# Local attention in the stream: two-bank reads, one exponent a tile, group products ahead of the scores

## What is computed

```python
x = x + attn_a(layernorm(x));  x = x + ffn(layernorm(x))
x = x + attn_b(layernorm(x));  x = x + ffn(layernorm(x))

def layer(x, wqkv, qs, ksc, wo, lg, lb, w1, b1, w2, b2):   # 8 heads of 64, window 64
    q, k, v = heads(shift_token(x) @ wqkv)
    q, k = rotary_xpos(l2norm(q) * qs, l2norm(k) * ksc)
    # each window of 64 queries sees its own 64 keys and the 64 before, masked
    attn = softmax(where(mask, -big, (8 * q) @ k.T))
    x = x + (attn @ v) @ wo
    h = layernorm(shift_token(x)) * lg + lb
    a, g = split(h @ w1 + b1)                               # 341 columns each
    return x + (a * gelu(g)) @ w2 + b2
```

## Time and profile before

| | |
|---|---|
| median of three runs | 1033.52 us |
| lowest and highest | 1033.38 and 1034.92 us |
| profiled execution, its own time | 1037.81 us |
| span of its trace | 1036.0 us |
| mean granted TensorE clock (share of full) | 0.979 |
| TensorE busy | 958.6 us (93%) |
| TensorE weight loads busy | 585.5 us (57%) |
| VectorE busy | 735.3 us (71%) |
| ScalarE busy | 736.7 us (71%) |
| GpSimd busy | 387.5 us (37%) |

### The profile page before, as it was taken

How to read it: one execution, slowest core, us unless ns; L and a number is a source line. 1 busy time by engine, 2 the same in 40 slices (tenths; PEclk the granted TensorE clock), 3 DMA queues, 4 the chain that set the end, 5 groups by cost and what they waited for, 6 DMA issues and landing times.

```text
span 1036.0 us, 22905 instructions
## 1 busy us (share of the span) xinstructions
PE 958.6 (93%) x8720; PEld 585.5 (57%) x8720; DVE 735.3 (71%) x1218; ACT 736.7 (71%) x1568; POOL 387.5 (37%) x270
## 2 busy tenths in 40 slices
PE   5999999998789999999998998989899999999985
PEld 2333333333576667666665566656666676666752
DVE  3787887884687877777776667757677777776741
ACT  3477777777587787877866675767668778787762
POOL 3010113000656545455443433424263553634410
PEclk9999999999899999999999998999999999999998
DMA  2200000000411101011010000000010100111100
GB/s 69 66 15 1 2 2 2 2 2 2 119 26 23 27 17 32 18 27 22 18 29 9 22 17 14 21 15 22 7 32 17 28 22 17 32 28 26 33 22 11
DMA packets 23303, 23.72 MB, mean 23 GB/s; under 512 B 8626, under 2 KB 15068, under 8 KB 23196
## 3 DMA queue, kind: packets, MB, share of 16 engines
q1 hardware_dynamic: 23196, 22.27, 9.1%
HBM read 6.16 MB, written 1.05 MB: 7 GB/s over the span
## 4 chain that ended last, share of the span: by engine, by line
PE 62%; DVE 7%; ACT 2%; issue 2%; POOL 2%; DVEq 0%; POOLq 0%
PE psum L1267 8%; PE psum L1236 5%; PE psum L1176 5%; PE psum L1197 5%; PE psum L1148 5%; PE psum L1138 5%; PE psum L1186 4%; PE psum L1275 4%; PE psum L1140 4%; PE psum L1139 4%; PE psum L1260 3%; PE psum L1209 2%; PE psum L1254 2%; PE psum L1161 2%; DVE f_PT L1530 2%
## 5 line engine op out<-in xcount | busy, mean ns | idle before, releaser
L1067 POOL TENSOR_TENSOR f_A<-f_A,f_BS 128x1024 f32<-128x1024 f32 x64 | 151.0, 2360 | 222.6 <-DVE f_BS L1506 222.4
L743 DVE TENSOR_REDUCE a_M<-psum 128x2 f32<-128x1024 f32 x128 | 155.6, 1222 | 41.0 <-PE psum L547 40.3
L1072 POOL TENSOR_TENSOR f_A<-f_A,f_RN 128x1024 f32<-128x1024 f32 x64 | 121.8, 1903 | 91.1 <-ACT f_RN L1398 87.4
L675 ACT ACTIVATE a_PT<-psum 128x1024 f32<-128x1024 f32 x128 | 128.7, 1023 | 24.9 <-PE psum L557 24.4
L1383 ACT ACTIVATE f_PW<-psum,f_NM 128x128 f32<-128x128 f32 x512 | 138.4, 380 | 4.2 <-DVE f_NM L1538 4.2
L1538 DVE TENSOR_REDUCE f_NM<-psum 128x4 f32<-128x512 f32 x128 | 82.3, 685 | 68.0 <-PE psum L1176 66.8
L1349 ACT ACTIVATE f_SQ<-psum 128x512 f32<-128x512 f32 x128 | 75.3, 608 | 71.5 <-PE psum L1140 67.0
L1502 DVE TENSOR_TENSOR f_A<-psum,cos 128x512 f32<-128x512 f32 x128 | 87.8, 686 | 45.2 <-ACT f_SQ L1349 45.1
L1197 PE MATMUL psum<-f_VS,f_PT 128*64 128x65 f32 x1024 | 81.2, 228 | 32.5 <-DVE f_hidden L1585 13.8
L1197 PEld LDWEIGHTS psum<-f_VS,f_PT 128*64 128x64 f32 x1024 | 67.8, 139 | 65.5 <-issue 48.4
L1267 PE MATMUL psum<-f_mid,f_w 128*128 128x512 f32 (+1 forms) x192 | 86.5, 601 | 2.7 <-DVE f_mid L1568 2.7
(11 more groups left out here) (191 smaller groups left out, 1948.7 us busy)
## 6 DMA issues: line engine op xcount, KB each, us to landing
f_VS<-f_V SPq DMA_DIRECT2D x112, 130.0 KB, 2.3
raw<-L_ffn_wqkv_dram SPq DMA_DIRECT2D x2, 768.0 KB, 5.4
a_XT<-L_attn_a_x_dram SPq DMA_DIRECT2D x4, 256.0 KB, 2.9
out_dram<-f_OUT SPq DMA_DIRECT2D x4, 256.0 KB, 2.3
f_w<-L_ffn_w_dram SPq DMA_DIRECT2D x2, 341.0 KB
tables<-const_dram SPq DMA_DIRECT2D x1, 512.0 KB, 3.8
f_wo<-L_ffn_wo_dram SPq DMA_DIRECT2D x8, 64.0 KB
const<-const_dram SPq DMA_DIRECT2D x1, 264.0 KB, 3.0
```

What stands on the lines that cost most here:

```text
L675: nc.scalar.activation(PT[:, i % 4, :, :], psum[:, pair("by_key", i), :], ACT.Exp, scale=float(DA) ** -0.5).then_inc(s("exped"), 1)
L743: nc.vector.tensor_reduce(M[:, quads % 2, t, 2 * j:2 * j + 2], psum[:, pair("scores", i), :], AX_X, ALU.max).then_inc(s("maxed"), 1)
L1067: nc.gpsimd.tensor_tensor(A[:, k % 2, :, :], A[:, k % 2, :, :], BS[:, k % 2, :, :], ALU.add)\
L1072: nc.gpsimd.tensor_tensor(x, x, RN[:, k % 2, :, None].to_broadcast([P, 2 * HW, DW]), ALU.mult)\
```

## The change

Four things are changed in the stream.

- Softmax: VectorE takes the maxima of both score banks in one instruction and then adds the negated maxima to the scores of both banks, into SBUF (f_PW). ScalarE computes the exponent of the whole tile in place, in one instruction of 1024 columns without a bias. The score banks come free when VectorE's addition is done.
- Copies: q and k transposed, and the two transposed banks of exponents, are each copied by one ScalarE instruction over two neighbouring banks. VectorE's copy (1530) is gone, and turn_p_2 with it. For this the bank list skips bank 7 where a pair would straddle the end (28 skips). q is kept in the same tile as k.
- Division: one reciprocal and one multiplication for both banks of sums, and one semaphore increment for a tile's sums.
- Order: w1, w2 and wo come before the scores on TensorE, turn_p before turn_o on TensorE and ScalarE, norm before w1 on ScalarE, and w1, wo and w2 before soften on VectorE. All three blocks of w1 are one stage again on VectorE.

```diff
-           ("turn_o", 3, of_tile), ("w1", 5, of_group), ("turn_p", 2, of_tile),
+           ("turn_p", 2, of_tile), ("turn_o", 3, of_tile),
...
+           ("w1", 5, of_group), ("w2", 6, of_group), ("wo", 3, of_group), ("scores", 1, of_tile),
...
+    def together(first, second):
+
+        if len(order) % BANKS == BANKS - 1:
+            order.append(None)
+        order.extend((first, second))
+
...
-            order += [("turned_q", i), ("turned_k", i)]
-        elif stage in ("scores", "sums", "keys_b", "tokens_b"):
-            order += [(stage, 2 * i), (stage, 2 * i + 1)]
-        elif stage in ("turn_p", "turn_p_2"):
-            order += [("turn_p", 2 * i + (stage == "turn_p_2"))]
+            together(("turned_q", i), ("turned_k", i))
+        elif stage in ("scores", "sums", "keys_b", "tokens_b", "turn_p"):
...
+    def two_banks(first, second):
+
+        x, y = bank(*first), bank(*second)
+        assert y == x + 1
+        return psum[:, x:y + 1, :]
...
-             "turned_q": ("qk_copied", lambda i: 2 * i + 1), "turned_k": ("qk_copied", lambda i: 2 * i + 2),
-             "scores": ("exped", lambda i: i + 1), "turn_p": (("p_copied", "p_copied_2"), lambda i: i // 2 + 1),
-             "sums": ("divided", lambda i: i + 1), "turn_o": ("o_copied", lambda i: i + 1),
+             "turned_q": ("qk_copied", lambda i: i + 1), "turned_k": ("qk_copied", lambda i: i + 1),
+             "scores": ("lowered", lambda i: i // 2 + 1), "turn_p": ("p_copied", lambda i: i // 2 + 1),
+             "sums": ("divided", lambda i: i // 2 + 1), "turn_o": ("o_copied", lambda i: i + 1),
...
-                def turn_p(u):
-                    pe.wait_ge(s("exped"), u + 1)
-                    dst = take("turn_p", u)
-                    for c in range(PAIRS):
-                        last = nc.tensor.transpose(dst[:, P * c:P * c + P], PW[:, u % 4, c, :], g.ident)
-                    last.then_inc(s("turned_p"), 1)
+                def turn_p(k):
+                    pe.wait_ge(s("exped"), k + 1)
+                    for u in (2 * k, 2 * k + 1):
+                        dst = take("turn_p", u)
+                        for c in range(PAIRS):
+                            last = nc.tensor.transpose(dst[:, P * c:P * c + P], PW[:, u % 4, c, :], g.ident)
+                        last.then_inc(s("turned_p"), 1)
...
-                        nc.scalar.activation(QT[:, k % 2, :, :],
-                                             psum[:, bank("turned_q", k), :].rearrange("p (c x) -> p c x", c=PAIRS),
-                                             ACT.Copy).then_inc(s("qk_copied"), 1)
-                        act.wait_ge(s("turned"), 2 * k + 2)
-                        nc.scalar.activation(KT[:, :, 2 * t:2 * t + 2, :],
-                                             psum[:, bank("turned_k", k), :].rearrange("p (c s x) -> p c s x",
-                                                                                       c=PAIRS, s=2),
+                        of_q = TILES + k % 2
+                        both = KT[:, :, :, :].rearrange("p c (u s) x -> p u c (s x)", s=2)
+                        both = both[:, of_q:t - 1:t - of_q, :, :] if t else both[:, of_q::-of_q, :, :]
+                        nc.scalar.activation(both,
+                                             two_banks(("turned_q", k), ("turned_k", k))
+                                             .rearrange("p w (c x) -> p w c x", c=PAIRS),
                                              ACT.Copy).then_inc(s("qk_copied"), 1)
...
-                        for u in (2 * i, 2 * i + 1):
-                            act.wait_ge(s("maxed"), u + 1)
-                            if u >= 4:
-                                act.wait_ge(s("turned_p"), u - 3)
-                            for c in range(PAIRS):
-                                last = nc.scalar.activation(PW[:, u % 4, c, :],
-                                                            psum[:, bank("scores", u), P * c:P * c + P], ACT.Exp,
-                                                            bias=NM[:, u % 4, c:c + 1])
-                            last.then_inc(s("exped"), 1)
+                        k = i
+                        act.wait_ge(s("lowered"), k + 1)
+                        of = slice(2 * (k % 2), 2 * (k % 2) + 2)
+                        nc.scalar.activation(PW[:, of, :, :], PW[:, of, :, :], ACT.Exp).then_inc(s("exped"), 1)
...
-                        u = 2 * i
-                        act.wait_ge(s("turned_p"), u + 1)
-                        if u >= 4:
-                            act.wait_ge(s("sums"), u - 3)
-                        nc.scalar.activation(PT[:, u % 4, :, :],
-                                             psum[:, bank("turn_p", u), :].rearrange("p (c x) -> p c x", c=PAIRS),
+                        k = i
+                        act.wait_ge(s("turned_p"), 2 * k + 2)
+                        if k >= 2:
+                            act.wait_ge(s("sums"), k - 1)
+                        nc.scalar.activation(PT[:, 2 * (k % 2):2 * (k % 2) + 2, :, :],
+                                             two_banks(("turn_p", 2 * k), ("turn_p", 2 * k + 1))
+                                             .rearrange("p j (c x) -> p j c x", c=PAIRS),
                                              ACT.Copy).then_inc(s("p_copied"), 1)
...
-                    elif stage == "turn_p_2":
-                        u = 2 * i + 1
-                        dve.wait_ge(s("turned_p"), u + 1)
-                        if u >= 4:
-                            dve.wait_ge(s("sums"), u - 3)
-                        nc.vector.tensor_copy(PT[:, u % 4, :, :],
-                                              psum[:, bank("turn_p", u), :].rearrange("p (c x) -> p c x", c=PAIRS))\
-                          .then_inc(s("p_copied_2"), 1)
                     elif stage == "soften":
-                        dve.wait_ge(s("scores"), i + 1)
-                        for u in (2 * i, 2 * i + 1):
-                            if u >= 4:
-                                dve.wait_ge(s("exped"), u - 3)
-                            nc.vector.tensor_reduce(
-                                NM[:, u % 4, :], psum[:, bank("scores", u), :].rearrange("p (c x) -> p c x", c=PAIRS),
-                                AX_X, ALU.max, negate=True).then_inc(s("maxed"), 1)
+                        k = i
+                        dve.wait_ge(s("scores"), k + 1)
+                        if k >= 2:
+                            dve.wait_ge(s("lowered"), k - 1)
+                        of = slice(2 * (k % 2), 2 * (k % 2) + 2)
+                        x = two_banks(("scores", 2 * k), ("scores", 2 * k + 1)).rearrange("p j (c x) -> p j c x", c=PAIRS)
+                        nc.vector.tensor_reduce(NM[:, of, :], x, AX_X, ALU.max, negate=True).then_inc(s("maxed"), 1)
+                        dve.wait_ge(s("maxed"), k + 1)
+                        if k >= 2:
+                            dve.wait_ge(s("turned_p"), 2 * k - 2)
+                        nc.vector.tensor_tensor(PW[:, of, :, :], x, NM[:, of, :, None].to_broadcast([P, 2, PAIRS, P]),
+                                                ALU.add).then_inc(s("lowered"), 1)
                     elif stage == "sums":
-                        for u in (2 * i, 2 * i + 1):
-                            x = psum[:, bank("sums", u), 0:PAIRS * (DW + 1)].rearrange("p (c x) -> p c x", c=PAIRS)
-                            dve.wait_ge(s("sums"), u + 1)
-                            nc.vector.reciprocal(RD[:, u % 4, :], x[:, :, DW]).then_inc(s("den_recip"), 1)
-                            dve.wait_ge(s("den_recip"), u + 1)
-                            if u >= 4:
-                                dve.wait_ge(s("turned_o"), u // 2 - 1)
-                            nc.vector.tensor_tensor(ON[:, u % 4, :, :], x[:, :, 0:DW],
-                                                    RD[:, u % 4, :, None].to_broadcast([P, PAIRS, DW]), ALU.mult)\
-                              .then_inc(s("divided"), 1)
+                        k = i
+                        of = slice(2 * (k % 2), 2 * (k % 2) + 2)
+                        x = two_banks(("sums", 2 * k), ("sums", 2 * k + 1))[:, :, 0:PAIRS * (DW + 1)]
+                        x = x.rearrange("p j (c x) -> p j c x", c=PAIRS)
+                        dve.wait_ge(s("sums"), k + 1)
+                        nc.vector.reciprocal(RD[:, of, :], x[:, :, :, DW]).then_inc(s("den_recip"), 1)
+                        dve.wait_ge(s("den_recip"), k + 1)
+                        if k >= 2:
+                            dve.wait_ge(s("turned_o"), k - 1)
+                        nc.vector.tensor_tensor(ON[:, of, :, :], x[:, :, :, 0:DW],
+                                                RD[:, of, :, None].to_broadcast([P, 2, PAIRS, DW]), ALU.mult)\
+                          .then_inc(s("divided"), 1)
```

66 lines of the change are left out of this document (33 added, 33 removed).

## The result

The changed kernel takes **1083.0 us** (median of 4 runs, 1082.66 to 1083.87) against 1033.5: ratio **1.0454**, 95% interval 1.0425 to 1.0483, slower. The forecast was 1063 us in a range of 1038 to 1085.

What follows compares the result with a forecast made beforehand. TensorE's list order was taken as the bound. Output steps +30.4, norm +6.5, up -9.7, linear-attention groups +2, fill and end +1 gave +30 us: 1068 profiled, 1063 as median; own range 1048 to 1076, whole range 1038 to 1085.

Steps and rivals of the forecast that it cites:

- the clock falls: Rival: most of the 8 long output-step stalls are each followed by a half-clock stretch, +14, 1077 us; chance 0.17.
- the linear groups get worse: Rival: each linear-attention group is +5 us through bank waits that chain, 1081 us; chance 0.08.
- What bounds it: TensorE's list order sets a plain group's time; work off ScalarE or VectorE is worth only what TensorE waits for it.
- Loop and output step: Scores to squares, then turn_o's copy: output product stalls 2.15 us, 3.2 behind a first layer's down step; +30.4 us in all.
- 1.2 us or less: Sign of being wrong: an output product that waits no longer than this for turn_o's copy.
- Norm and up steps: Plain groups: norm steps slower by 1.0 (5) or 0.25 (6), +6.5 us; up steps -0.5 (4) or -1.1 (7), -9.7 us.
- the down step: Down step of plain groups: no change, 0, as f_hidden is ready and the exponents end before turn_p's place.
- The end with its last plain group: End of the stream: the forecast gave the fill and the end together about +1 us.
- The linear-attention groups: Four groups: old waits and half clock go, new waits of 8 us against 7.5 before; +0.5 each, +2 us.
- The faster one: Rival: waits go, nothing replaces them, output product waits only 1.2 us, linear groups -6.4 each; -32, 1002 us; chance 0.13.

Runs made afterwards that it cites:

- experiment 1: All new operations, with the engine lists in the order of the kernel before and turn_p whole in front of the scores: 1039.25 us, 1.0032 to before.
- 2: Kernel before with its old operations, in the new order of the changed kernel: 1041.56 us, ratio 1.0050 to before.
- 7: New operations in the old order, with ScalarE's squares ahead of the exponents: 1031.42 us, ratio 0.9964 to the kernel before.
- 9: Kernel before with its own operations; on VectorE alone the tokens' division and all of w1 moved ahead of the maxima: 1023.25 us, ratio 0.9857.
- 8: New operations in the old order, squares ahead of the exponents, and VectorE's division of the tokens ahead of the maxima: 1020.08 us, 0.9848 to the kernel before.

## Why the prediction was right, and where its size was off

- **Direction and mechanism right, size too small.** +29.5 us were forecast and +49.5 measured. The time lies 2 us inside the upper bound of the range (1085) and outside the forecast's own, 1048 to 1076. By the time alone the rivals "the clock falls" (1077) and "the linear groups get worse" (1081) fit better; the lengths of the steps and the list of waits are what speaks for the forecast.
- **What bounds it.** Right. TensorE's list order set the time; 56 us taken off ScalarE bought nothing, and the 47 us of experiment 1, in the old order, bought nothing either. The prediction had allowed this up to 45 us of gain, at 0.02. (ScalarE's work fell by 0.88 us a tile where 0.7 was said, VectorE's rose by 0.26 where 0.2 was said.)
- **Loop and output step.** Right in mechanism and size. The exponents were to be ready at 3.6 us behind a first layer's down step, and were at 3.62; turn_o's copy at 7.65, and ended at 7.40; 3.05 and 2.0 us more a step were said, 3.0 and 2.1 measured. The loss isn't one wait of 3.2 us at the product, as the text had it: turn_p and, every other time, turn_o wait for the loop before the product does, and the product itself waits 1.24 or 2.24 us. So its signs were set too coarsely: 2 to 3.3 us each was said for the product's waits, and five of the eight came to 1.21 or 1.24, next to the "1.2 us or less" that it gave as a sign of being wrong.
- **Norm and up steps.** Right by type: +1.16 or nothing, and -0.43 or -1.18, against 1.0 or 0.25 and -0.5 or -1.1. In the ten plain groups five norm steps and five up steps are of the dearer kind.
- **The terms of the sum that were too small.** The ten plain groups, by the predicted step types (8 x 3.05 + 2 x 2.0, 5 x 1.0 + 5 x 0.25, 4 x -0.5 - 6 x 1.1), make 26 us, and 31.8 came. 1.7 of the difference is the output step of 15.07 us, in which the clock fell. 1.3 is the first output step, +3.3 for +2.0, whose mean clock was 0.88 and not 1.00. 1.0 is the output step right behind the linear-attention groups, +4.0 for +3.05, in which the projection (L1151) waits 2.59 us for a bank whose reader is Y, a wait I hadn't walked there. 1.8 is the down step, predicted at 0 and 0.13 to 0.19 longer in most; its cause stays open. The end with its last plain group gave +5.2 for about +2; in it TensorE once waits 2.6 us for the exponents (L1200), which the kernel before never does there.
- **The linear-attention groups** gave +3.8 for +2. Two of the four down steps, 16.3 us instead of 14.6, hold a half-clock stretch; that is 3.4 us. The term was also added up wrongly: what goes was put at 7.5 us a group, but the waits and the half clock that the text names make 18.9 / 4 + 1.7 = 6.4, the number that its own rival uses. With 6.4 the term would have been +6. What covered the slip is that the new waits came to 6.9 us a group (1.49, 2.24, 1.63, 1.18 and 0.35 in the second) and not 8; that part of the forecast was near by luck.
- **The two that are no part of the change.** 4.6 us lie ahead of the first plain group, nearly all of it ahead of the stream, where no instruction was changed (below). And I took the profiled execution's 4.3 us above the median as something that would be so again: the changed kernel's profiled run was 1083.18 with a median of 1083.0. The two make 9 of the 20 us between forecast and result; plain groups, linear groups and the end make the other 11.
- **What a measurement tells.** The prediction put it at 0.2%. The kernel before alone had medians from 1033.5 to 1036.95 us, 0.3% apart, and single runs from 1032.3 to 1048.0. For the change itself this doesn't matter; for experiments 1, 2 and 7 it is the size of the effect.
- **The rivals.** The faster one fell with its condition: where the output product waits only 1.2 us, the stages before it wait 1.2 us or more themselves, and elsewhere it waits 2.0 to 2.24. "The clock falls" happened in one of the eight long output steps, not in most. The linear groups got worse by 1 us each, not by 5.
- **What I believed and the runs denied.** That the order alone carried the loss (expected 1066, measured 1041.6), and that the operations alone would gain (expected 1015, measured 1039). The walk through the lists got the usual steps of a plain group of the changed kernel within 0.25 us, but was never made for either half, where other things come last.

## What to carry to other kernels

In a loop over engines that run fixed lists, ask for each link what other work lies beside it; an edit that lengthens the loop by 1 us and one that takes the work away from beside it can each cost next to nothing (0.3 and 0.5% here), and 4.5% together. Before merging small instructions into large ones, count when the first result is ready and what waits behind the large one, not the busy time saved. And look first at who stands behind whom in the queue of the engine that is waited for: moving one division and one block of w1 ahead of the maxima gained 1.4% in the kernel before, with no operation changed.

## What the runs showed of the hardware

- ScalarE's exponent of 1024 columns takes 1060 ns from SBUF to SBUF, and the copy of 1024 from PSUM 1032 to 1034 (the groups above). The first phase's exponent of 1024 columns from PSUM takes 1023, so reading from SBUF gained nothing.
- VectorE's addition of 1024 columns with one PSUM operand takes 1224 ns, as long as the maxima over the same columns, 1221.
- Equal stalls don't always cost the clock. Behind the three stalls of the step from 408.96 it stood at 0.68 while the output product ran; behind the same three in the step from 500.69 it stayed at 1.00. TensorE was busy for 2.75 of the 5.20 us before the product in both:

```profile
411.20:416.40 5.20, 2.75 (x21) 2.03 (x19) 4.33 (x8) 4.83 (x7) 1.34 (x2) 1.00 0.22 49
416.40:421.70 5.30, 5.30 (x8) 2.01 (x8) 0.37 (x1) 0.83 (x3) 3.64 (x2) 0.68 0.02 5
502.93:508.13 5.20, 2.75 (x22) 2.02 (x20) 4.33 (x8) 4.83 (x7) 1.34 (x2) 1.00 0.22 50
508.13:511.83 3.70, 3.70 (x12) 1.51 (x16) 0.36 (x1) 0.83 (x3) 3.56 (x2) 1.00 0.01 2
714.30:717.72 3.42, 3.42 (x5) 1.35 (x4) 0.00 (x0) 1.31 (x4) 0.84 (x2) 0.50 0.00 0
```

  It made that step 1.7 us longer (15.07 against 13.37). In the same way all four down steps of the linear-attention groups have one wait of 2.24 us for the new x (L1267); in the last two a stretch at half clock follows it (the last row), in the first two none does, and those with it take 16.3 us instead of 14.6. So waits shorter than the 3.5 us of the earlier trace rows can be followed by the lower clock, and no row here tells which will be.
- The first phase, whose code is the same in all these kernels, isn't equally long in them: the first step of the stream starts at 258.0 us in experiment 1, 259.9 in 9, 261.1 in the kernel before, 264.1 in 8 and 265.7 in the changed one, whose clock stood at 0.83 between 120 and 160 us (0.96 before). The clock doesn't explain the order: over the first 258 us it was lowest in experiment 1 (0.94), which was through first, and 1.00 in both 8 and 9. The cause stays open. Differences of less than some 8 us between two single profiles prove nothing here; step lengths do.
